# First two pairs of a 32-pair pipeline: W1 loaded first, adapters taken pair by pair, x2 ahead of the Q/K/V remainders

## The chip, the cores and the metric

One core of a Trainium2 chip. The metric is the device time of one execution in microseconds. The kernel before has a median of 950.8 over three runs (950.08 to 954.0).

## The reference

Four residual layers on x, 64 sequences of 64 tokens with 512 features, all in 32-bit floats. Only the first three matter here:

```python
x = x + einsum('bsi,bio->bso', x, W0[id]) + b0[id]           # one expert of 16 for each sequence
x = x + einsum('btd,od->bto', x, W1)                          # W1 and a low-rank adapter,
      + einsum('btr,bor->bto', einsum('btd,brd->btr', x, A[ad]), B[ad]) * s[ad]
x = x + attention(x)      # Q, K, V projections, RMS norm, rotation, a window of 256 old keys from a paged cache, Wo
x = x + einsum('bct,bcd->bdt', x, W3[subject]) + b3
```

## The kernel before

Two sequences make a pair of 128 rows, and 32 pairs go through two phases. Phase one computes the first two layers and Q, K and V, and stores x2, q and the new key and value rows; phase two does the attention and the last layer. Each engine has its own program, written out by hand, and runs it strictly in that order; semaphores tie them together. The first four pairs of phase one are written out without a loop.

In phase one, step k of an engine's program works on pair k and on the later parts of pair k-1 and k-2. For a pair:

- SP loads the two expert matrices, x, the bias and the rotation rows (`load_in`, for pair 0 `load_first`). All are issued on SP's one queue, in the order of the code. The loads of pair k wait for the expert products and the x1 of pair k-2.
- PE multiplies with the experts (`experts`, L602) into a bank. GpSimd (POOL) has summed x and bias (`sum_x_bias`, L461), and VectorE (DVE) adds both to x1 (`add_x1`, L1200).
- PE transposes x1 (L706). ScalarE (ACT) rounds it to x1t_hi (L926) and copies it to x1t (L927); DVE forms the remainder x1t_lo (L1234). A product with full precision is made of three: hi with hi, hi with lo, lo with hi.
- PE multiplies x1t with the two adapters' A (`adapt_down`, L623); ACT rounds that to xa_hi (L937) and DVE forms xa_parts (L1245). Then come the three W1 products (L728), four matmuls each, and one product with the adapters' B (L732), for which ACT has rounded pair_b to pair_b_hi (`round_adapters`, L893) and DVE has split it (`split_adapters`, L1212).
- DVE adds the sum to x1, which gives x2 (L1276). In the next step PE transposes x2 (L612), ACT rounds it (L919), DVE forms x2t_lo (L1205), and PE multiplies with the rounded Q, K and V weights and their remainders (L654 to L666).
- ACT squares q and k (L963, L964) and copies v; DVE sums, POOL takes the power (rms, L471), DVE and POOL rotate, PE transposes q.

ACT also loads pair_b and builds pair_a for a pair (`take_adapters`, L879 and L882): in the loop for pair k+2 at the end of step k. For pairs 0 and 1 it issues all four loads of pair_b ahead of step 0, behind the rounding of W1. Weights come into `stage` and are split once: ACT rounds W1 (L872) and Q, K, V (L942, L945), DVE forms the remainders w1_lo (L1229) and wqkv_lo (`split_inputs`, L1217). Before step 0 DVE also computes indices, the key bounds (L1074 to L1079) and the gains for the rotation tables (L1080 to L1084).

POOL's sum for the third pair (step 2) stands in step 2 behind the power and the rotation of the second; for later pairs it stands one step ahead.

`warm_up` (L584) are dummy matmuls of PE ahead of the first work and between its first pieces.

Of the kernel before, what the change touches and what calls it, by code (L numbers as in the profile page):

```python
# [4 lines left out]
F32 = mybir.dt.float32  # L5
# [43 lines left out]
WARM, WARM_X, WARM_T, WARM_Q, WARM_KEYS = 9, 6, 6, 24, 26  # L49
# [10 lines left out]
def build(nc, a):  # L60

    ctx = ExitStack()
    with ctx:
# [213 lines left out]
        def _(sp):  # L277

            sp.dma_start(ids_sb[:, :, :], a["ids"]).then_inc(ld_ids, 16)
            sp.dma_start(xt[:, 0, :, :], a["xt"][0]).then_inc(ld_xt[0], 16)  # L280
            sp.wait_ge(ld_ids, 16)
# [19 lines left out]
            def load_first():  # L301
# [15 lines left out]
                sp.dma_start(w1_stage, a["w1"]).then_inc(ld_w1, 16)  # L317
                sp.dma_start(lora_a[:, :, :], a["la"]).then_inc(ld_la, 16)
                sp.dma_start(wqkv_stage[:, :, 0:D], a["wq"]).then_inc(ld_wq, 16)
                sp.dma_start(wqkv_stage[:, :, D:D + 256], a["wk"]).then_inc(ld_wkv, 16)  # L320
                sp.dma_start(wqkv_stage[:, :, D + 256:], a["wv"]).then_inc(ld_wkv, 16)
                for h in range(2):
                    p0 = sp.value_load(ids_sb[0:1, 2, h:h + 1], min_val=0, max_val=NSLOT * BLK - T)
                    sp.dma_start(cs[T * h:T * h + T, 0, :], a["rope"][bass.ds(p0, T), :]).then_inc(ld_rope, 16)

# [249 lines left out]
        def _(pe):  # L575
# [51 lines left out]
            def project_inputs(k, s):  # L627

                if isinstance(k, int) and k == NP:
# [4 lines left out]
                    for ps_out, n0, done in ((ps_kv, D, kv_done), (ps_q, 0, qkv_done)):  # L634
# [7 lines left out]
                        last.then_inc(done, 1)  # L642
                elif on(k, 1, NP):
# [4 lines left out]
                    if isinstance(k, int) and k == 1:  # L648
                        pe.wait_ge(w_hi_ready, 2)
                    for ps_out, n0 in ((ps_q, 0), (ps_kv, D)):  # L650
                        if isinstance(k, int) and k == 1 and n0 == D:
                            pe.wait_ge(w_hi_ready, 3)
# [3 lines left out]
                    if isinstance(k, int) and k == 1:  # L656
                        pe.wait_ge(wqkv_lo_ready, 1)
                    for ps_out, n0 in ((ps_q, 0), (ps_kv, D)):
                        if n0 == D and on(k, 0, NP) and not (isinstance(k, int) and k == 1):
                            adapt_down(k, s)  # L660
                        if isinstance(k, int) and k == 1 and n0 == D:
                            pe.wait_ge(wqkv_lo_ready, 2)
# [17 lines left out]
            def phase_one(k, j, s):  # L680
# [35 lines left out]
                if on(k, 0, NP):  # L716

                    if isinstance(k, int) and k < 2:
                        adapt_down(k, s)
# [5 lines left out]
                    pe.wait_ge(x1lo_ready, k + 1)  # L725
                    for x_part, w_part in ((x1t_hi, w1_hi), (x1t_hi, w1_lo), (x1t_lo, w1_hi)):
                        for c in range(DC):
# [140 lines left out]
        def _(act):  # L868
            act.dma_start(numbers[:, :], a["numbers"]).then_inc(ld_small, 16)
            act.dma_start(reals[:, :], a["reals"]).then_inc(ld_small, 16)  # L870
            act.wait_ge(ld_w1, 16)
            nc.scalar.activation(w1_hi[:, :, :], w1_stage, ACT.Copy).then_inc(w_hi_ready, 1)  # L872

# [39 lines left out]
            def phase_one(k, j, s):  # L913
                r = 1 - s
                if on(k, 1, NP):
# [3 lines left out]
                    nc.scalar.activation(x2t_hi[:, :, :].rearrange("p c t -> p (c t)"), ps_t2[:, :], ACT.Copy).then_inc(x2hi_ready, 1)  # L919
                if on(k, 2, NP) and not (isinstance(k, int) and k == NP):  # L920
# [7 lines left out]
                if isinstance(k, int) and k == 0:  # L928
                    act.wait_ge(ld_la, 16)
                    for n in range(2):  # L930
                        take_adapters(n, n, load=False)
                    round_adapters(0, 0, 0)
# [5 lines left out]
                if on(k, -1, NP):  # L938
                    round_adapters(k + 1, j + s, 1 - s)
                if isinstance(k, int) and k == 0:  # L940
                    act.wait_ge(ld_wq, 16)
                    nc.scalar.activation(wqkv_hi[:, :, 0:D], wqkv_stage[:, :, 0:D], ACT.Copy).then_inc(w_hi_ready, 1)  # L942
                if isinstance(k, int) and k == 0:
                    act.wait_ge(ld_wkv, 2 * 16)
                    nc.scalar.activation(wqkv_hi[:, :, D:], wqkv_stage[:, :, D:], ACT.Copy).then_inc(w_hi_ready, 1)  # L945
# [22 lines left out]
                if on(k, -2, NP):  # L968
# [67 lines left out]
        def _(dve):  # L1036
# [37 lines left out]
            link(V.tensor_scalar(first_key[:, :], kvl_row[:, :], -1.0, float(WIN), ALU.mult, ALU.add))  # L1074
            link(V.tensor_scalar(first_key[:, :], first_key[:, :], fcols[:, TCOL:TCOL + 1], None, ALU.max))
            link(V.tensor_scalar(odd_i[:, :], kvl_row[:, :], 1, None, ALU.bitwise_and))
            link(V.tensor_scalar(odd[:, :], odd_i[:, :], 1.0, None, ALU.mult))
            link(V.tensor_tensor(first_key[:, :], first_key[:, :], odd[:, :], ALU.subtract))
            link(V.tensor_scalar(beyond[:, :], odd[:, :], BIG, None, ALU.mult))  # L1079
            link(V.tensor_scalar(gain_in[:, :, :], gain_in[:, :, :], 1.0, None, ALU.add))  # L1080
            for w, g in ((0, -1.0 / 16.0), (1, 1.0)):
                for f, half, sign in ((0, 0, 1.0), (1, 1, 1.0), (2, 1, -1.0), (3, 0, 1.0)):
                    link(V.tensor_scalar(gains[:, w, f, :], gain_in[:, w, 32 * half:32 * half + 32], g * sign, None, ALU.mult))
            V.tensor_copy(scol[:, 4:5], scol[:, 3:4]).then_inc(gains_ready, 1)  # L1084
# [351 lines left out]
```

## Time and profile before

| | us |
|---|---|
| median of three runs | 950.8 (950.08 to 954.0) |
| span of the profiled execution | 948.6 |
| PE busy | 907.5 (96%) |
| DVE busy | 651.1 (69%) |
| POOL busy | 522.3 (55%) |
| ACT busy | 444.3 (47%) |

Phase one ends at about 510 us of the profiled execution. Times in the rows are counted from the start of its span. Lines are those of the kernel before; behind a tile's name stands what it is made from. ACTq and SPq are instructions of the engine's own queue, mostly issues of loads. A bracket at the end of a row of the timeline tells how long the engine was idle ahead of it and what released it.

### The profile page before, as it was taken

To read this page: it belongs to the slowest core of one execution; us is meant where nothing else is said; L and a number is where in the kernel's file an instruction comes from. 1 tells how busy PE (TensorE), PEld (TensorE's weight loads), DVE (VectorE), ACT (ScalarE), POOL (GpSimd) and SP (SyncE) were. 2 spreads that over 40 slices of the span, in tenths; PEclk is the share of its full clock that TensorE was granted. 3 is DMA by queue.
4 is the path that set the end of the run, shared out by engine and by line. 5 is a ranking of instruction groups with operands and counts; after the bars stand their busy time and mean duration, and the time that the engine had idled before them with its cause. 6 is when DMAs were issued, how large, how long until landed. Compare 5 with 4: busy or idle time off the path is not lost.

```text
span 948.6 us, 23332 instructions
## 1 busy us (share of the span) xinstructions
PE 907.5 (96%) x6477; PEld 660.8 (70%) x6477; DVE 651.1 (69%) x1853; ACT 444.3 (47%) x1190; POOL 522.3 (55%) x502
## 2 busy tenths in 40 slices
PE   5789999999999999999997899999999999999997
PEld 3456666766666667666676777877777887787785
DVE  5345545667768774556754678777878877888875
ACT  2333333333333333333322566666666666666663
POOL 2136455464564657855556666566565665656530
PEclk9799999999999999999998799999999999999999
DMA  9978988778788787887844566666666676567741
GB/s 295 265 230 282 330 308 290 252 261 289 247 282 276 244 291 255 271 295 247 284 159 152 183 188 203 199 210 186 198 197 212 200 225 203 181 209 212 221 135 46
DMA packets 100413, 218.51 MB, mean 230 GB/s; under 512 B 30187, under 2 KB 36168, under 8 KB 92178
## 3 DMA queue, kind: packets, MB, share of 16 engines
q1 hardware_dynamic: 66290, 145.27, 47.0%
q0 software_dynamic: 25088, 57.74, 20.5%
q10 hardware_dynamic: 8992, 15.00, 4.9%
q8 instruction: 18, 0.29, 0.1%
q14 instruction: 25, 0.20, 0.1%
HBM read 210.39 MB, written 33.86 MB: 257 GB/s over the span
## 4 chain that ended last, share of the span: by engine, by line
PE 51%; POOL 18%; issue 15%; DMA 7%; SPq 4%; DVE 2%; ACT 1%; ACTq 1%; POOLq 0%; DVEq 0%
PE banks L823 9%; PE banks L775 9%; PE banks L811 7%; PE banks L798 6%; POOL rms L471 5%; DMA ring<-in_rope 5%; PE banks L752 4%; PE banks L859 3%; POOL ring L475 3%; POOL x_in L461 3%; PE banks L816 3%; POOL q_rot L480 2%; PE banks L753 1%; PE banks L791 1%; POOL ring L482 1%
## 5 line engine op out<-in xcount | busy, mean ns | idle before, releaser
L561 POOL DMA_INDIRECT ring<-new_rows,idx x128 | 129.4, 1011 | 82.5 <-PE banks L775 40.3
L471 POOL TENSOR_TENSOR rms<-ss,neg_half 128x12 f32<-128x12 f32 x31 | 70.8, 2284 | 185.4 <-DVE ss L1259 185.4
L992 ACT ACTIVATE big<-big,neg_max 128x320 f32<-128x320 f32 x256 | 141.4, 554 | 3.1 <-DVE neg_max L1317 2.7
L1317 DVE CUSTOM_DVE_ANT_0 big<-banks,mask 128x320 f32<-128x320 f32 x256 | 114.6, 486 | 27.4 <-PE banks L775 26.0
L602 PE MATMUL banks<-ring 128*64 128x512 f32 x512 | 117.8, 601 | 0.9 <-DMA ring<-in_w 0.9
L982 ACT ACTIVATE kt<-banks 128x384 f32<-128x384 f32 x128 | 61.8, 483 | 97.5 <-PE banks L753 97.5
L775 PE MATMUL banks<-kt,q_in 64*128 64x128 f32 (+2 forms) x768 | 88.6, 364 | 1.3 <-ACT kt L982 1.3
L550 POOL DMA_INDIRECT ring<-new_rows,idx x64 | 61.7, 965 | 47.0 <-PE banks L798 42.7
L1354 DVE TENSOR_SCALAR big<-big,recip 128x320 f32<-128x320 f32 x256 | 85.5, 396 | 2.3
L775 PEld LDWEIGHTS banks<-kt,q_in 64*128 64x128 f32 x768 | 74.4, 189 | 14.4 <-issue 8.4
L811 PEld LDWEIGHTS banks<-pt,ring 128*64 128x64 f32 x1024 | 55.4, 136 | 38.1 <-DVE pt L1299 25.4
L602 PEld LDWEIGHTS banks<-ring 128*64 128x64 f32 x512 | 34.1, 137 | 67.6 <-issue 66.8
L919 ACT ACTIVATE x2t_hi<-banks 128x512 fp32r<-128x512 f32 x32 | 19.1, 598 | 128.0 <-PE banks L612 128.0
L514 POOL DMA_INDIRECT ring<-in_kvrows,idx x64 | 61.2, 956 | 28.8 <-issue 13.5
L811 PE MATMUL banks<-pt,ring 128*64 128x128 f32 x1024 | 70.0, 278 | 2.7 <-DVE pt L1299 2.3
L664 PE MATMUL banks<-wqkv_hi,x2t_lo 128*128 128x512 f32 x248 | 70.4, 405 | 0.0
L798 PE MATMUL banks<-ident,big 128*128 128x128 f32 x512 | 67.4, 275 | 0.4 <-DVE ot_lo L1306 0.4
L654 PE MATMUL banks<-wqkv_hi,x2t_hi 128*128 128x512 f32 x248 | 66.6, 412 | 0.7 <-ACT x2t_hi L919 0.7
L666 PE MATMUL banks<-wqkv_lo,x2t_hi 128*128 128x512 f32 x248 | 66.6, 390 | 0.0
L1234 DVE TENSOR_TENSOR x1t_lo<-x1t,x1t_hi 128x512 fp32r<-128x512 f32 x32 | 40.3, 1258 | 35.9 <-ACT x1t L927 35.9
L1200 DVE TENSOR_TENSOR x<-banks,x_in 128x512 f32<-128x512 f32 x32 | 22.1, 691 | 55.6 <-PE banks L602 50.9
L798 PEld LDWEIGHTS banks<-ident,big 128*128 128x128 f32 x512 | 58.5, 142 | 1.0 <-DVE ot_lo L1306 0.9
(177 smaller groups left out, 1989.0 us busy)
## 6 DMA issues: line engine op xcount, KB each, us to landing
ring<-in_w SPq DMA_DIRECT2D x62, 1024.0 KB, 7.5
ring<-in_xt SPq DMA_DIRECT2D x32, 256.0 KB, 2.7
x_in<-in_x SPq DMA_DIRECT2D x32, 256.0 KB, 5.8
bias_in<-in_b SPq DMA_DIRECT2D x64, 128.0 KB, 6.4
x_dram<-x SPq DMA_DIRECT2D x32, 256.0 KB, 6.9
q_dram<-q_t ACTq DMA_DIRECT2D x32, 256.0 KB, 5.7
new_rows<-kv_out SPq DMA_DIRECT2D x32, 256.0 KB, 6.7
q_in<-q_dram SPq DMA_DIRECT2D x32, 256.0 KB, 2.7
```

The costliest lines, as they stand in the source:

```text
L471: nc.gpsimd.tensor_tensor(rms[:, s, :], ss[:, s, :], neg_half[:, :], ALU.pow).then_inc(rms_ready, 1)
L561: pool.indirect_dma_start(out=kv[:, s, c, :], out_offset=None, in_=new_rows, in_offset=bass.IndirectOffsetOnAxis(ap=idx[:, b, 1 + c:2 + c] ...
L602: last = nc.tensor.matmul(ps_l0[T * h:T * h + T, :], xt[:, s, c, T * h:T * h + T], w0[:, 2 * s + h, c * D:(c + 1) * D], start=(c == 0), st ...
L654: nc.tensor.matmul(ps_out[:, :], x2t_hi[:, c, :], wqkv_hi[:, c, n0:n0 + D], start=(c == 0), stop=False)
L664: nc.tensor.matmul(ps_out[:, :], x2t_lo[:, c, :], wqkv_hi[:, c, n0:n0 + D], start=False, stop=False)
L775: return nc.tensor.matmul(banks[:, S0[g] + n0:S0[g] + n1], q_in[r0:r0 + HD, s % 4, g // 2, :], kt[r0:r0 + HD, s % 2, g // 2, k0 + n0:k0 + ...
L798: last = nc.tensor.transpose(ps_pt[p][:, (q * 2 + c) * P:(q * 2 + c + 1) * P], prob[:, r % 2, (5 * p + 3 * q + c) * P:(5 * p + 3 * q + c + ...
L811: nc.tensor.matmul(ps_o[p][HD * q:HD * q + HD, :], kv[:, r, c, v0:v0 + HD], pt[:, p, PLACE[2 * p + q] % 2, c, :], start=(c == 0), stop=Fal ...
L823: last = nc.tensor.matmul(out[:, n0:n1], o_part[:, pair_s, c, :], w_part[:, c, n0:n1], start=(c == 0 and n == 0), stop=(c == DC - 1 and n ...
L992: nc.scalar.activation(prob[:, s % 2, PLACE[g] * NK:(PLACE[g] + 1) * NK], sm[:, s % 2, g, :], ACT.Exp, bias=neg_max[:, s % 2, g:g + 1], sc ...
L1317: V.tensor_tensor_reduce(sm[:, s % 2, g, :], ps_s[g], mask[:, s % 2, k0:k0 + NK], 1.0, 3.0e38, ALU.add, ALU.min, accum_out=neg_max[:, s % ...
L1354: V.tensor_scalar(own_row, own_row, recip[:, s % 2, g:g + 1], None, ALU.mult).then_inc(prob_ready, 1)
```

## The change

It touches the first pairs alone; the loop and phase two stay as they are.

- SP: W1's load is issued right behind the first x^T, ahead of the wait for the ids and of the expert weights. The rotation rows of pair 0 go ahead of K and V.
- ACT: the pair_b loads of pair 0 alone are issued at the start, then W1 is rounded, then pair 0's pair_b. In step 0 pair_a is built for pair 0 alone, and the Q weights are rounded ahead of xa_hi. In step 1, behind x2t_hi, ACT rounds K and V, loads and builds the adapters of pair 1 and rounds them, and loads and builds those of pair 2, all ahead of pair 1's x1t_hi.
- DVE: w1_lo goes ahead of the first x1; the key bounds move to step 3; the gains move into step 0 behind x1t_lo. Both weight splits and pair 1's adapter split move from step 0 behind x2t_lo in step 1, so x2 of pair 0 no longer stands behind them.
- PE: for pairs 0 and 1 the W1 products of x1t_hi come ahead of `adapt_down`, which comes ahead of those of x1t_lo. For pair 0's Q, K and V the products with the rounded weights come first and those with the remainders last. There are fourteen warm-up matmuls at the start instead of nine, and three instead of six behind the first x1 transposes.

DVE, from pair 0's x1 to its x2 and the remainder behind it (x is first x1, later x2), before:

```order
L1200 TENSOR_TENSOR x<-banks,x_in 128x512
L1229 TENSOR_TENSOR w_lo<-stage,w_hi 128x2048
L1234 TENSOR_TENSOR x1t_lo<-x1t,x1t_hi 128x512
L1212 TENSOR_TENSOR pair_b_parts<-pair_b,pair_b_hi 128x512
L1245 TENSOR_TENSOR xa_parts<-banks,xa_hi 64x64 x2
L1212 TENSOR_TENSOR pair_b_parts<-pair_b,pair_b_hi 128x512
L1217 TENSOR_TENSOR wqkv_lo<-stage,wqkv_hi 128x4x512
L1276 TENSOR_TENSOR x<-banks,x 128x512
L1205 TENSOR_TENSOR x2t_lo<-banks,x2t_hi 128x512
```

DVE in the same place, after, up to pair 1's x1 (the last row):

```order
L1216 TENSOR_TENSOR x<-banks,x_in 128x512
L1228 TENSOR_TENSOR pair_b_parts<-pair_b,pair_b_hi 128x512
L1251 TENSOR_TENSOR x1t_lo<-x1t,x1t_hi 128x512
L1096 TENSOR_SCALAR reals<-reals 128x128
L1099 TENSOR_SCALAR gains<-reals 128x32 x8
L1100 COPY scol<-scol 128x1
L1262 TENSOR_TENSOR xa_parts<-banks,xa_hi 64x64 x2
L1291 TENSOR_TENSOR x<-banks,x 128x512
L1221 TENSOR_TENSOR x2t_lo<-banks,x2t_hi 128x512
L1233 TENSOR_TENSOR wqkv_lo<-stage,wqkv_hi 128x4x512 x2
L1228 TENSOR_TENSOR pair_b_parts<-pair_b,pair_b_hi 128x512
L1216 TENSOR_TENSOR x<-banks,x_in 128x512
```

The second pair_b_parts (pair 1's) and the weight remainders moved from ahead of pair 0's x2 to behind it and ahead of pair 1's x1; the gains stand between x1t_lo and xa_parts.

ACT, step 1, from pair 0's x2t_hi to the squares of its q, before:

```order
L919 ACTIVATE x2t_hi<-banks 128x512
L926 ACTIVATE x1t_hi<-banks 128x512
L927 ACTIVATE x1t<-banks 128x512
L937 ACTIVATE xa_hi<-banks,reals 128x64
L893 ACTIVATE pair_b_hi<-pair_b,reals 128x512
L963 ACTIVATE sq<-banks 128x512
```

ACT from the same x2t_hi, after, through the first of four loads and builds of adapters, two for pair 1 and, behind pair 1's pair_b_hi, two for pair 2:

```order
L927 ACTIVATE x2t_hi<-banks 128x512
L930 ACTIVATE wqkv_hi<-stage 128x4x512
L883 TENSOR_LOAD ids_sb
L883 ISA x2
L885 ISA
L885 DMA pair_b<-in_lb 48x512
L888 ISA
L888 ACTIVATE pair_a<-lora_a,reals 128x4x48
```

ACT, after, from the last of these four to the squares:

```order
L885 DMA pair_b<-in_lb 48x512
L888 ISA
L888 ACTIVATE pair_a<-lora_a,reals 128x4x48
L940 ACTIVATE x1t_hi<-banks 128x512
L941 ACTIVATE x1t<-banks 128x512
L951 ACTIVATE xa_hi<-banks,reals 128x64
L899 ACTIVATE pair_b_hi<-pair_b,reals 128x512
L971 ACTIVATE sq<-banks 128x512
```

Between x2t_hi and x1t_hi there now stand the K/V rounding, four adapter loads with their builds, and a wait for the first two of them; pair 2's pair_b_hi, which stood ahead of the squares and still does, now takes loads that are issued in this same step.

The core of the diff:

```diff
-WARM, WARM_X, WARM_T, WARM_Q, WARM_KEYS = 9, 6, 6, 24, 26
+WARM, WARM_X, WARM_T, WARM_Q, WARM_KEYS = 14, 6, 3, 24, 26
...
             sp.dma_start(xt[:, 0, :, :], a["xt"][0]).then_inc(ld_xt[0], 16)
+            sp.dma_start(w1_stage, a["w1"]).then_inc(ld_w1, 16)
             sp.wait_ge(ld_ids, 16)
...
-                    if isinstance(k, int) and k < 2:
-                        adapt_down(k, s)
                     wait(pe, x2_ready, k)
...
                     for x_part, w_part in ((x1t_hi, w1_hi), (x1t_hi, w1_lo), (x1t_lo, w1_hi)):
+                        if isinstance(k, int) and k < 2 and x_part is x1t_lo:
+                            adapt_down(k, s)
+                            pe.wait_ge(x1lo_ready, k + 1)
...
             act.wait_ge(ld_ids, 16)
+            act.wait_ge(pb_set, 2)
+            take_adapters(0, 0, copy=False)
+            act.wait_ge(ld_w1, 16)
+            nc.scalar.activation(w1_hi[:, :, :], w1_stage, ACT.Copy).then_inc(w_hi_ready, 1)
             act.wait_ge(ld_small, 2 * 16)
-            act.wait_ge(pb_set, 2)
-            for k in range(2):
-                take_adapters(k, k, copy=False)
+            round_adapters(0, 0, 0)
...
+                if isinstance(k, int) and k == 1:
+                    act.wait_ge(ld_wkv, 2 * 16)
+                    nc.scalar.activation(wqkv_hi[:, :, D:], wqkv_stage[:, :, D:], ACT.Copy).then_inc(w_hi_ready, 1)
+                    take_adapters(1, 1)
+                    round_adapters(1, 0, 1)
+                    take_adapters(2, 0)
...
                 if isinstance(k, int) and k == 1:
                     split_x2(k)
+                    split_inputs(0)
                     split_inputs(1)
+                    split_adapters(1, 1)
...
                     if isinstance(k, int) and k == 0:
-                        split_adapters(0, 0)
+                        make_gains()
```

## Rows read from the trace of the kernel before

**Rows 1.** PE's waits, 60 to 505 us: total us, times, longest

```profile
PE banks L612 <- DVE x L1276: 2.2, 1, 2.2
PE banks L677 <- POOL q_rot L480: 2.1, 9, 0.6
```

**Rows 2.** Stretches: length, PE busy (instructions), granted clock, DMA share, GB/s

```profile
4.00:6.00 2.00, 1.59 (x7) 1.00 0.81 210
6.00:12.00 6.00, 5.19 (x21) 1.00 1.02 363
24.10:27.40 3.30, 3.30 (x12) 0.50 1.04 303
36.80:41.10 4.30, 4.30 (x10) 0.50 1.05 306
48.20:51.30 3.10, 1.14 (x20) 1.00 0.34 85
55.00:72.70 17.70, 15.74 (x87) 1.00 0.84 258
200.00:300.00 100.00, 99.14 (x544) 1.00 0.85 271
```

**Rows 3.** Timeline of PE, start and length in us, instruction, [idle before <-releaser]

```profile
17.21 0.66 PE L706 MATMUL banks<-ident,x 128*128 128x128 f32 x4 [1.70 <-DVE x L1200]
...
28.52 0.39 PE L732 MATMUL banks<-pair_b_parts,xa_parts 128*128 128x512 f32 x1
34.99 1.11 PE L612 MATMUL banks<-ident,x 128*128 128x128 f32 x4 [6.08 <-DVE x L1276]
...
50.82 0.69 PE L623 MATMUL banks<-x1t,pair_a 128*64 128x64 f32 x16 [1.22 <-issue]
...
56.24 3.65 PE L602 MATMUL banks<-ring 128*64 128x512 f32 x16
...
62.88 0.66 PE L706 MATMUL banks<-ident,x 128*128 128x128 f32 x4 [1.96 <-DVE x L1200]
```

**Rows 4.** Timeline of DVE

```profile
13.58 2.76 DVE L1083 TENSOR_SCALAR gains<-reals 128x32 f32<-128x32 f32 x8
...
30.12 0.69 DVE L1212 TENSOR_TENSOR pair_b_parts<-pair_b,pair_b_hi 128x512 fp32r<-128x512 f32 x1 [2.45 <-ACT pair_b_hi L893]
31.92 2.29 DVE L1217 TENSOR_TENSOR wqkv_lo<-stage,wqkv_hi 128x2048 fp32r<-128x2048 f32 x1 [1.11 <-ACT wqkv_hi L942]
34.24 0.69 DVE L1276 TENSOR_TENSOR x<-banks,x 128x512 f32<-128x512 f32 x1
```

**Rows 5.** Timeline of ACT and its queue (ACTq)

```profile
18.05 3.45 ACTq L879 DMA_DIRECT2D pair_b<-in_lb  x4
21.54 0.60 ACT L926 ACTIVATE x1t_hi<-banks 128x512 fp32r<-128x512 f32 x1 [2.56 <-issue]
...
29.36 0.72 ACT L893 ACTIVATE pair_b_hi<-pair_b,reals 128x512 fp32r<-128x512 f32 x1 [2.59 <-DMA pair_b<-in_lb]
29.99 1.89 ACT L942 ACTIVATE wqkv_hi<-stage 128x2048 fp32r<-128x2048 f32 x1
30.05 1.50 ACTq L879 DMA_DIRECT2D pair_b<-in_lb  x2
...
51.75 0.71 ACT L893 ACTIVATE pair_b_hi<-pair_b,reals 128x512 fp32r<-128x512 f32 x1
```

**Rows 6.** Timeline of POOL

```profile
14.61 1.26 POOL L461 TENSOR_TENSOR x_in<-x_in,bias_in 128x512 f32<-128x512 f32 x1 [5.97 <-DMA bias_in<-in_b]
...
60.78 1.26 POOL L461 TENSOR_TENSOR x_in<-x_in,bias_in 128x512 f32<-128x512 f32 x1
```

**Rows 7.** Landing of pair_b loads (L879): that issued at 31.2; all 17 to 130

```profile
DMA to landing us min/median/max: 8.2/8.2/8.2
...
DMA to landing us min/median/max: 5.0/6.2/8.2
```

**Rows 8.** Landing of the expert matrix (L292) issued at 22.8

```profile
DMA to landing us min/median/max: 14.1/14.1/14.1
```

More of the change, by code:

```diff
@@ L642, in project_inputs @@
                         last.then_inc(done, 1)
+                elif isinstance(k, int) and k == 1:
+                    pe.wait_ge(x2hi_ready, 1)
+                    for i, (ps_out, n0) in enumerate(((ps_q, 0), (ps_kv, D))):
+                        pe.wait_ge(w_hi_ready, 2 + i)
+                        for c in range(DC):
+                            nc.tensor.matmul(ps_out[:, :], x2t_hi[:, c, :], wqkv_hi[:, c, n0:n0 + D], start=(c == 0), stop=False)
+                        pe.wait_ge(x2lo_ready, 1)
+                        for c in range(DC):
+                            nc.tensor.matmul(ps_out[:, :], x2t_lo[:, c, :], wqkv_hi[:, c, n0:n0 + D], start=False, stop=False)
+                    for i, (ps_out, n0) in enumerate(((ps_q, 0), (ps_kv, D))):
+                        pe.wait_ge(wqkv_lo_ready, 1 + i)
+                        for c in range(DC):
+                            last = nc.tensor.matmul(ps_out[:, :], x2t_hi[:, c, :], wqkv_lo[:, c, n0:n0 + D], start=False, stop=(c == DC - 1))
+                    last.then_inc(qkv_done, 1)
                 elif on(k, 1, NP):
@@ L929, in phase_one @@
                     act.wait_ge(ld_la, 16)
-                    for n in range(2):
-                        take_adapters(n, n, load=False)
-                    round_adapters(0, 0, 0)
+                    take_adapters(0, 0, load=False)
+                    act.wait_ge(ld_wq, 16)
+                    nc.scalar.activation(wqkv_hi[:, :, 0:D], wqkv_stage[:, :, 0:D], ACT.Copy).then_inc(w_hi_ready, 1)
                 if on(k, 0, NP):
@@ L937, in phase_one @@
                     nc.scalar.activation(xa_hi[:, :], ps_la[:, 0:T], ACT.Copy, scale=fcols[:, XPART:XPART + 1]).then_inc(xa_hi_ready, 1)
-                if on(k, -1, NP):
+                if on(k, -1, NP) and not (isinstance(k, int) and k == 0):
                     round_adapters(k + 1, j + s, 1 - s)
[L940 to L945, printed above, removed]
                 if on(k, 2, NP) and not (isinstance(k, int) and k == NP):
@@ L967, in phase_one @@
                     nc.scalar.activation(kv_out[:, r, 256:512], ps_kv[:, 256:512], ACT.Copy).then_inc(sqv_ready, 1)
-                if on(k, -2, NP):
+                if on(k, -2, NP) and not (isinstance(k, int) and k == 0):
                     take_adapters(k + 2, s)
@@ L1073, in _ @@
                 link(V.tensor_scalar(xa_parts[T * h:T * h + T, T - T * h:P - T * h], mrow[T * h:T * h + T, 0:T], 0.0, None, ALU.mult))
[L1074 to L1083, printed above, removed]
@@ L1086, in take_tables, with make_gains @@
+            def make_gains():
+                link(V.tensor_scalar(gain_in[:, :, :], gain_in[:, :, :], 1.0, None, ALU.add))
+                for w, g in ((0, -1.0 / 16.0), (1, 1.0)):
+                    for f, half, sign in ((0, 0, 1.0), (1, 1, 1.0), (2, 1, -1.0), (3, 0, 1.0)):
+                        link(V.tensor_scalar(gains[:, w, f, :], gain_in[:, w, 32 * half:32 * half + 32], g * sign, None, ALU.mult))
+                V.tensor_copy(scol[:, 4:5], scol[:, 3:4]).then_inc(gains_ready, 1)
             def take_tables():
@@ L1246, in phase_one @@
                     last.then_inc(xa_ready, 1)
-                if on(k, -1, NP):
+                if on(k, -1, NP) and not (isinstance(k, int) and k == 0):
                     split_adapters(k + 1, r)
-                if isinstance(k, int) and k == 0:
-                    split_inputs(0)
                 if isinstance(k, int) and k == NP:
```

35 lines of the change are left out of this document (16 added, 19 removed).

## The prediction

> **What bounds the kernel now.** I read the waits of the tensor engine (PE) first, then its busy time and granted clock by stretch, then the timelines of the first 63 us on each engine, then the landing times of single loads. From 60 to 505 us PE waits 2.2 us on one x2 add and 2.1 us in nine small waits on q_rot [rows 1], and from 200 to 300 us it is busy 99.14 of 100 us at full clock [rows 2]. So phase one is bound by PE once it runs, and a microsecond won or lost before that reaches the end of phase one as it is. The loads, the attention phase and the stores behind it hang on PE's progress, and nothing there has a date of its own. The question is only when the steady run begins. Its first instruction is the transpose of the third pair's x1 at 62.88, before which PE stood 1.96 us for the DVE add [rows 3]; from there it does not stop. I follow what sets that date.
>
> Two stretches come before it. **The first pair's x2** is added at 34.24, though its last product L732 started at 28.52 and took 0.39 [rows 3, 4]. In between DVE stood in program order behind pair 1's split (30.12, after 2.45 us of waiting for ACT's rounding, which itself waited for a load until 29.36) and behind a 2.29 us weight split [rows 4, 5]. **The third pair's start** is late for another reason: from the ACT rounding of pair 2's adapter at 51.75 a chain of ACT squares, DVE sums, the POOL power and rotation, and POOL's x + bias at 60.78 leads to 62.88 without a gap that the change touches [rows 5, 6]. That chain is 62.88 - 51.75 = 11.1 us long, and it stays.
>
> **The change, part by part.** W1's load goes ahead of the expert weights. It is 128 x 2048 words, 1.05 MB; at the 363 GB/s of 6 to 12 us that would hold the rest back by 2.9 us, but from 4 to 6 us only 210 GB/s moved [rows 2], so 0.3 MB (0.85 us) fits into room that is empty now, and it is issued before the wait for the ids. Ends: 0 and 2.9 us; I take 1.7. The bias then lands at 16.3 instead of 14.6, and POOL's sum of 1.26 [rows 6] ends at 17.55. Against it DVE no longer has the gains in front of x1: the row from 13.58 is 2.76 us long [rows 4] and ended about half a microsecond after POOL's sum did. Pair 0's x1 is added at 17.6, and its transposes start at 18.35 instead of 17.21 [rows 3]: a loss of 1.1 us.
>
> Then the gain begins. ACT issued four adapter loads, 3.45 us from 18.05, and was late with x1t_hi because of that: it rounded at 21.54 after transposes that ended at 17.9 [rows 3, 5]. After the change two loads were issued long before; x1t_hi runs from 19.05 to 19.65. PE takes the eight rounded W1 products at once; twelve such products took some 3.3 us at half clock [rows 2], so at full clock they are no bound. DVE has x1t_lo until about 20.9 and then the moved gains, 2.76 plus about 0.4 for the instruction on each side, to 24.1. ACT rounds the Q weights in 1.89 us [rows 5], is done by about 23.3, and has xa_hi at 23.6. So xa_parts waits for the gains: the cover that hid them is gone and they cost about half a microsecond here. xa_parts at 24.1 to 24.6, L732 0.39 [rows 3], x2 added from 25.05 to 25.75: **9.2 us earlier than 34.24** [rows 4]. The transposes end at 26.5.
>
> This is not what reaches the end. Pair 1's adapter loads, issued before 21.5 now, move behind x2t_hi and the K/V rounding on ACT, so they start from that 26.5. When ACT was released at 29.36, the two loads behind it took 1.50 us from 30.05 [rows 5], so the second was issued at 31.2, 1.85 us after the release. Here: 28.35. That load landed after 8.2 us [rows 7], with the same queue of expert weights ahead of it as it will have here, so pair 1's pb_hi can start at 36.55. Behind this wait stand, on ACT, the loads for pair 2, x1t_hi of pair 1 and all that follows; on DVE, pair 1's split and its x1 add. Pair 2's second load then goes out 1.85 us after 36.55, at 38.4. Of seventeen such loads the shortest took 5.0, the median 6.2 and the longest 8.2 [rows 7]; the queue is still loaded then, so I take 7.0, between median and longest. Pair 2's rounding starts at 45.4 instead of 51.75: **6.3 us earlier**. The chain of 11.1 us brings the steady start to 56.5.
>
> By the Trainium skill (DMA: Bandwidth & Descriptors, "Queues, rings and completion order"), each DMA engine takes turns between the queue rows that have work, a packet from each, so a small load on ACT's row should not stand behind what SP has queued; the same page's "Anatomy of one DMA — SWDGE (gpsimd) path" puts the fixed cost at about 2 us. By that the two landings would be an estimated 2 to 3 us each and this chain no bound at all. The trace disagrees with 5.0 as the shortest of 17 and 8.2 beside a full SP queue.
>
> The other path to pair 2's rounding is PE's. Pair 1's second expert matrix was issued at 22.8 and landed 14.1 us later, at 36.9 [rows 8]; the earlier start of the queue brings that to about 35.4. Q/K/V of pair 0 are ready before that: rounding K/V from 26.6 takes two times 1.89 at most, the two splits on DVE 2.29 each [rows 4, 5], which gives about 33. Expert products 3.65 [rows 3], x1, transposes, x1t_hi, eight W1 products and the adapter product: xa_hi at 44.0. That is 1.4 us before the landing, so it is not the later one, but it is the floor: faster loads gain at most 51.75 - 44.0 = 7.75 us.
>
> What is late next is PE's clock. Pair 2's expert products, from 56.24 now, will be done by about 49.5, and until 56.5 PE has eight transposes. The clock was full from 55 to 72.7. From 48.2 to 51.3 PE was busy 1.14 us, and behind that the clock stood at its lower level (1.2 instead of 2.4 GHz); the unbroken work from 24.1 to 27.4 and from 36.8 to 41.1 also ran at 0.50 before the clock rose [rows 2]. Half of such a stretch is lost, 1.65 to 2.15 us; I take 1.8. Bounds 0 (it does not fall) and 2.15.
>
> The rest costs nothing: the key bounds move to step 3, where DVE waits for ACT's xa_hi anyway; W1's remainder split fits behind the index arithmetic, before x1; fourteen warm-ups instead of nine lie inside the later landing of the expert weights; three fewer behind the transposes free PE for x1t_hi; rope ahead of K/V moves 0.07 MB. Sum: -6.3 + 1.8 = **-4.5 us**. The profiled execution goes from a span of 948.6 to 944.1, and since the median of the three runs is 950.8, 2.2 above that span, I predict 946.3. A half per cent is 4.75 us, about what a measurement of this kernel can tell from no change.
>
> **The rivals.** Short landings: the adapter loads take the trace's shortest times, sum near 11 instead of 15.2. PE's path then binds (from a sum of 13.8 down), -7.75 + 1.8 = -5.95, 944.9. The turn-taking in the Trainium skill's page on DMA would end here too. For this rival speaks that ACT's queue is its own; against it the 8.2 [rows 7]. No fall of the clock: -6.3, 944.5; against it the fall after 48.2. A later x2: the W1 load holds the first pair back by its full 2.9 us (1.2 more) and both landings are at 8.2 (1.2 more), -2.1, 948.7. Slower: the two adapter landings are in series where they were issued ahead of need, and each delays ACT and through it everything. The gain is gone when their sum is 15.2 + 4.5 = 19.7 us and half a per cent is lost at 24.4, 12 us each (955.5). The longest seen is 8.2 for one, but large SP loads took 14.1 in the same stretch [rows 8]. That the change does not reach the end at all (phase one bound elsewhere) has PE's 99.14 of 100 us against it and is part of the slow case.
>
> **How the numbers follow.** Forecast 0.45, short landings 0.18, clock stays 0.07, later x2 0.22, slower 0.08. The forecast lies 0.25 us inside the half per cent, so a little under half of it counts as faster: 0.20 + 0.18 + 0.07 = 0.45 faster; 0.25 + 0.22 + 0.02 = 0.49 same; 0.06 slower. The range runs from PE's floor with the clock kept (-7.75: 943.0) to a gain of 0.8 (950.0), which leaves out most of the slower case and the tail of the later x2.
>
> **What would show it.** Right: x1t_hi of pair 0 near 19 and its x2 near 25; ACT idle until about 36.5 before pair 1's pb_hi, and again until about 45.4 before pair 2's, both released by the pair_b load; POOL's power following by some 3 us; PE with a hole of several us before the third pair's x1 transposes and half clock behind it; then no wait of PE over 1 us in phase one. Wrong: pb_hi released by PE or by nothing, no hole ahead of the third pair, or PE waiting again later in phase one.

## The result and the profile after

The kernel after the change takes 943.9 us (median of four times, 941.1 to 944.8). The four times of the kernel before on record beside it have a median of 950.8, 7.0 us more; the ratio on record is 0.9908 [0.9881, 0.9935], which is 8.7 us, 6.2 to 11.3. A second comparison (a2_after) gives 942.2 against 953.0, 0.9887 [0.9863, 0.9912], 10.8 us. The forecast was 946.3, a gain of 4.5. The time lies in the range, at its lower end; the gain is 1.6 to 2.4 times the forecast, and "no change that can be measured" had the larger share of the chances. The profiled span went from 948.6 to 941.5, by 7.1.

The start of the kernel after, first POOL's first sum (start and length in us, instruction, [idle before <-releaser]), which answers to the first of [rows 6]:

```profile
16.28 1.27 POOL L461 TENSOR_TENSOR x_in<-x_in,bias_in 128x512 f32<-128x512 f32 x1 [7.88 <-DMA bias_in<-in_b]
```

DVE, where the gains now stand (beside [rows 4]):

```profile
17.65 0.69 DVE L1216 TENSOR_TENSOR x<-banks,x_in 128x512 f32<-128x512 f32 x1 [3.73 <-POOL x_in L461]
...
21.07 1.69 DVE L1099 TENSOR_SCALAR gains<-reals 128x32 f32<-128x32 f32 x8
...
24.02 0.69 DVE L1291 TENSOR_TENSOR x<-banks,x 128x512 f32<-128x512 f32 x1 [0.60 <-PE banks L741]
```

ACT and its queue, from the first pair's x2t_hi to the third pair's adapter (beside [rows 5]):

```profile
25.45 0.60 ACT L927 ACTIVATE x2t_hi<-banks 128x512 fp32r<-128x512 f32 x1 [2.52 <-PE banks L612]
...
26.13 1.51 ACTq L885 DMA_DIRECT2D pair_b<-in_lb  x2
...
34.73 0.72 ACT L899 ACTIVATE pair_b_hi<-pair_b,reals 128x512 fp32r<-128x512 f32 x1 [6.19 <-DMA pair_b<-in_lb]
35.75 0.33 ACTq L885 DMA_DIRECT2D pair_b<-in_lb  x1
...
36.93 0.33 ACTq L885 DMA_DIRECT2D pair_b<-in_lb  x1
...
41.59 0.31 ACT L951 ACTIVATE xa_hi<-banks,reals 128x64 fp32r<-128x64 f32 x1 [2.40 <-PE banks L623]
44.11 0.72 ACT L899 ACTIVATE pair_b_hi<-pair_b,reals 128x512 fp32r<-128x512 f32 x1 [2.20 <-DMA pair_b<-in_lb]
```

The two new waits are there, 6.19 and 2.20 us, both released by the pair_b load, and the second one sets the date: the xa_hi of the same engine is through by 41.9. The four loads, and a fifth issued at 44.79, landed in 6.7 to 7.4 us:

```profile
DMA to landing us min/median/max: 6.7/7.2/7.4
```

PE, first the second pair's expert products, then the third pair (beside the end of [rows 3]):

```profile
32.98 3.65 PE L602 MATMUL banks<-ring 128*64 128x512 f32 x16 [0.56 <-DMA ring<-in_w]
...
49.82 0.66 PE L612 MATMUL banks<-ident,x 128*128 128x128 f32 x4 [2.54 <-DVE x L1291]
51.86 1.11 PE L684 MATMUL banks<-ident,q_rot 128*128 128x128 f32 x4 [1.38 <-POOL q_rot L480]
55.23 1.12 PE L713 MATMUL banks<-ident,x 128*128 128x128 f32 x4 [2.26 <-DVE x L1216]
...
66.59 3.65 PE L602 MATMUL banks<-ring 128*64 128x512 f32 x16
```

and its stretches there (length, PE busy with instructions, granted clock, DMA share, GB/s), beside [rows 2]:

```profile
4.00:6.00 2.00, 1.76 (x8) 1.00 0.94 375
6.00:12.00 6.00, 3.86 (x26) 1.00 1.00 355
48.00:52.00 4.00, 0.80 (x5) 0.95 1.00 297
52.00:56.00 4.00, 1.74 (x8) 0.50 0.22 68
56.00:60.00 4.00, 4.00 (x15) 0.69 0.88 274
60.00:64.00 4.00, 4.00 (x31) 1.00 1.03 352
```

The third pair's x1 transposes moved from 62.88 to 55.23, by 7.65 us. In front of them PE is busy 0.80 of 4 us and then 1.74 of 4, and the clock goes to its lower level (1.2 instead of 2.4 GHz) for about 7 us (0.50 in every microsecond from 52 to 58, and parts of the two beside them). The expert products of the fourth pair, the first work behind that stretch, moved from 72.74 to 66.59, by 6.15; so the clock took 1.50 back. Behind it PE waits as little as before [rows 1]: from 60 to 505 us

```profile
PE banks L612 <- DVE x L1291: 2.2, 1, 2.2
PE banks L684 <- POOL q_rot L480: 2.2, 10, 0.4
PE banks L639 <- ACT x2t_hi L927: 0.7, 1, 0.7
```

### The profile page after: what moved, and what is told of

It is laid out like the page before. It is cut to its first block, busy times and chain, and to the rows that moved or that the text cites. A ratio compares the mean times of both kernels' runs of the same rounds, so it can differ in the third digit from the quotient of the medians.

```text
span 941.5 us, 23334 instructions
## 1 busy us (share of the span) xinstructions
PE 901.8 (96%) x6481; PEld 655.9 (70%) x6481; DVE 649.5 (69%) x1853; ACT 445.2 (47%) x1190; POOL 520.1 (55%) x502
## 4 chain that ended last, share of the span: by engine, by line
PE 52%; POOL 20%; issue 15%; DMA 5%; SPq 2%; DVE 2%; ACT 1%; ACTq 0%; POOLq 0%; DVEq 0%
PE banks L832 9%; PE banks L784 9%; PE banks L820 7%; PE banks L807 6%; POOL rms L471 6%; PE banks L761 4%; POOL ring L475 3%; PE banks L868 3%; POOL x_in L461 3%; POOL q_rot L480 3%; PE banks L825 3%; DMA ring<-in_rope 2%; DMA pair_b<-in_lb 2%; PE banks L671 2%; POOL ring L494 1%
## 5 line engine op out<-in xcount | busy, mean ns | idle before, releaser
L561 POOL DMA_INDIRECT ring<-new_rows,idx x128 | 129.4, 1011 | 81.6 <-PE banks L784 45.4
L820 PEld LDWEIGHTS banks<-pt,ring 128*64 128x64 f32 x1024 | 55.3, 136 | 38.3 <-DVE pt L1314 26.1
L514 POOL DMA_INDIRECT ring<-in_kvrows,idx x64 | 61.2, 956 | 28.7 <-issue 13.5
L671 PE MATMUL banks<-wqkv_hi,x2t_lo 128*128 128x512 f32 x240 | 67.9, 404 | 0.0
L673 PE MATMUL banks<-wqkv_lo,x2t_hi 128*128 128x512 f32 x240 | 64.4, 390 | 0.0
L665 PE MATMUL banks<-wqkv_hi,x2t_hi 128*128 128x512 f32 x240 | 64.0, 409 | 0.0
```

What stands on the lines that cost most here:

```text
L561: pool.indirect_dma_start(out=kv[:, s, c, :], out_offset=None, in_=new_rows, in_offset=bass.IndirectOffsetOnAxis(ap=idx[:, b, 1 + c:2 + c] ...
L671: nc.tensor.matmul(ps_out[:, :], x2t_lo[:, c, :], wqkv_hi[:, c, n0:n0 + D], start=False, stop=False)
L673: last = nc.tensor.matmul(ps_out[:, :], x2t_hi[:, c, :], wqkv_lo[:, c, n0:n0 + D], start=False, stop=(c == DC - 1))
L820: nc.tensor.matmul(ps_o[p][HD * q:HD * q + HD, :], kv[:, r, c, v0:v0 + HD], pt[:, p, PLACE[2 * p + q] % 2, c, :], start=(c == 0), stop=Fal ...
```

## The experiments

All dates come from one profile of each kernel. A span falls into four pieces in every one of these traces: the start, up to the fourth pair's expert products; the steady run, up to the transposes of the last x2; the turn into phase two, up to the eighth transposes of keys (L752 before, L761 after); and the rest. Over all fourteen traces the steady run takes 427.3 to 428.2 us and the rest 410.0 to 410.5. The turn takes 34.9 to 40.3, and two traces of one kernel differ there by up to 2.5. So a change in the first pairs is read at the first two columns, and the span carries the turn's scatter besides.

| kernel | third pair's x1 transposes | fourth pair's experts | turn | span |
|---|---|---|---|---|
| before, as shown | 62.88 | 72.74 | 38.0 | 948.6 |
| before, b2_before | 66.52 | 76.37 | 35.9 | 950.5 |
| before, b3_before | 65.93 | 77.41 | 38.4 | 954.0 |
| after, as shown | 55.23 | 66.59 | 37.6 | 941.5 |
| after, a2_after | 54.89 | 66.76 | 38.3 | 942.6 |
| e1_loads_early | 55.33 | 68.00 | 34.9 | 940.8 |
| e2_sum_ahead | 53.17 | 64.04 | 37.1 | 939.2 |
| e3_fill | 55.20 | 65.04 | 35.7 | 938.4 |
| e4_x2_late | 57.31 | 69.59 | 38.4 | 945.6 |
| e5_before_dve | 65.09 | 76.38 | 40.3 | 955.2 |
| e6_w1_back | 60.86 | 73.24 | 36.2 | 947.4 |
| e8_loads_step0 | 53.92 | 65.96 | 38.3 | 941.7 |
| e9_step0_sum | 51.41 | 61.20 | 39.7 | 939.1 |
| e9b_step0_sum | 50.78 | 60.57 | 40.1 | 938.6 |

My theory: the landings of the adapter loads, one after the other on ACT, set the third pair's date; a fixed chain of about 11 us and the clock follow. The rivals: PE's own path or the x2 of the first pair sets it, or the order on DVE alone does.

**The loads issued early.** All four loads for the first two pairs go out at the start again, the rest of the change stays:

```diff
-            take_adapters(0, 0, copy=False)
+            for k in range(2):
+                take_adapters(k, k, copy=False)
...
-                    take_adapters(1, 1)
+                    take_adapters(1, 1, load=False)
...
-                    take_adapters(2, 0)
...
```

The loads for pair 2 go back to the end of step 0, behind a wait for the first split.

> The changed kernel with one part undone: ACT issues the pair_b loads of pairs 0 and 1 together at the start, and those of pair 2 at the end of step 0, as before the change; the rest of the change stays. Theory (two adapter landings in series set the third pair's start): ACT no longer waits for a load in step 1; pair 2's pb_hi follows xa_hi of pair 1 at about 41.8 instead of 44.1, PE's x1 transposes of the third pair start near 53 instead of 55.2, and the span falls by about 2 us. Rival (the loads were not the bound, taking them pair by pair is what won time because ACT's queue is short): the x1 transposes at 55.2 or later, span the same or longer.

Both adapter waits went, and the date did not move (55.33). ACT in this kernel:

```profile
30.10 0.71 ACT L899 ACTIVATE pair_b_hi<-pair_b,reals 128x512 fp32r<-128x512 f32 x1
43.99 0.31 ACT L951 ACTIVATE xa_hi<-banks,reals 128x64 fp32r<-128x64 f32 x1 [2.40 <-PE banks L623]
44.20 0.71 ACT L899 ACTIVATE pair_b_hi<-pair_b,reals 128x512 fp32r<-128x512 f32 x1
```

and PE's second expert products, which started at 32.98 in the kernel after:

```profile
35.37 3.65 PE L602 MATMUL banks<-ring 128*64 128x512 f32 x16 [1.29 <-DMA ring<-in_w]
```

The last rounding now comes right behind xa_hi, at 44.20 instead of 44.11. The 0.2 MB of adapters ahead of the bias and the expert weights moved POOL's first sum from 16.28 to 17.79 and the second experts by 2.4 us. The expectation counted only the wait that goes, and not what the loads hold up: PE's path came in at the same date. This run alone doesn't tell the theory from its first rival; the next ones do.

**The loads issued in step 0.** Here the loads for pair 1 stand at the end of step 0, behind the first pair's loads but ahead of its x2:

```diff
-                if on(k, -2, NP) and not (isinstance(k, int) and k == 0):
+                if isinstance(k, int) and k == 0:
+                    take_adapters(1, 1)
+                elif on(k, -2, NP):
                     take_adapters(k + 2, s)
...
```

In step 1 those for pair 2 follow a wait for the first split and stand ahead of pair 1's rounding.

> The changed kernel with the adapter loads moved one place ahead on ACT without touching the start: pair 1's are issued at the end of step 0, behind xa_hi, where ACT stands idle from 22.9 to 25.4, and pair 2's behind the K/V rounding, ahead of the wait for pair 1's. The first loads stay as changed. Theory (the second landing is the bound of the third pair's start, and what kept the run with the loads at the very start from winning was 0.2 MB more ahead of the first bias): x1 of pair 0 stays at 17.65, pb_hi of pair 2 starts right behind xa_hi of pair 1 at 41.8 instead of 44.1, PE's x1 transposes of the third pair near 52.9 instead of 55.2, the span about 2 us shorter. Rival (ACT's own order or the issue of loads eats it): 55 or later.

The date came 1.3 us earlier (53.92). ACT:

```profile
24.55 0.33 ACTq L885 DMA_DIRECT2D pair_b<-in_lb  x1
...
33.99 0.72 ACT L899 ACTIVATE pair_b_hi<-pair_b,reals 128x512 fp32r<-128x512 f32 x1 [5.26 <-DMA pair_b<-in_lb]
42.59 0.31 ACT L951 ACTIVATE xa_hi<-banks,reals 128x64 fp32r<-128x64 f32 x1 [2.40 <-PE banks L623]
42.80 0.71 ACT L899 ACTIVATE pair_b_hi<-pair_b,reals 128x512 fp32r<-128x512 f32 x1
```

The second landing is off the path (42.80 right behind xa_hi), as the theory has it, and PE's path is the next bound, 1.3 us below. Here too that path came later than in the kernel after, with the second experts at 33.97 instead of 32.98, and of the 1.3 us 0.6 are left at the fourth pair's experts (65.96 against 66.59). Of pair 1's two loads the second went out 2.75 us earlier than in the kernel after (24.55 against 27.3) and was there only 0.74 earlier: 9.4 us instead of 7.4. The first, also 2.75 us earlier (23.38 against 26.13), kept most of its lead: 7.2 instead of 6.9.

**x2 late again.** The Q/K/V remainder goes back ahead of the first pair's x2:

```diff
                     split_x2(k)
-                    split_inputs(0)
                     split_inputs(1)
...
+                if isinstance(k, int) and k == 0:
+                    split_inputs(0)
```

> The changed kernel with one part undone on DVE: the split of the Q weights goes back ahead of pair 0's x2. That delays x2 by about 1.7 us (the split takes 2.3, and its weights are rounded at 22.7). Theory (x2, the issue of the adapter loads behind it, two landings and the POOL chain are one series): the third pair's x1 transposes start 1.7 us later, near 56.9, and the span is 1.7 us longer than the changed kernel's. Rival (there is slack behind x2): they start within 0.5 us of 55.2.

ACT, x2t_hi of the first pair and pair 1's rounding:

```profile
27.29 0.60 ACT L927 ACTIVATE x2t_hi<-banks 128x512 fp32r<-128x512 f32 x1 [4.44 <-PE banks L612]
...
37.94 0.72 ACT L899 ACTIVATE pair_b_hi<-pair_b,reals 128x512 fp32r<-128x512 f32 x1 [7.57 <-DMA pair_b<-in_lb]
```

x2t_hi came 1.84 us later (27.29), pair 1's rounding waited 7.57 us for its load until 37.94, and the third pair's date is 57.31, 2.08 later. So x2 counts by way of what ACT issues behind it.

**The order on DVE alone**, in the kernel before: both splits moved behind x2t_lo, nothing else.

```diff
                     split_x2(k)
+                    split_inputs(0)
                     split_inputs(1)
+                    split_adapters(1, 1)
...
-                if on(k, -1, NP):
+                if on(k, -1, NP) and not (isinstance(k, int) and k == 0):
                     split_adapters(k + 1, r)
-                if isinstance(k, int) and k == 0:
-                    split_inputs(0)
```

> The kernel before with one part of the change alone: on DVE the Q weight split and pair 1's adapter split go behind x2t_lo, so that pair 0's x2 no longer stands behind them. Theory (x2 early is of use only with ACT's order changed as well): x2 is added near 29.0 instead of 34.2, but x2t_hi stands on ACT behind the Q and K/V rounding and the builds for pair 2 until about 34.5 (36.1 before), so the third pair's x1 transposes start near 61.2 instead of 62.9 and the span falls by 1.6 us. Rival (the DVE order alone carries the gain): they start near 57 or earlier.

DVE, x2 and the remainder behind it:

```profile
31.80 0.69 DVE L1276 TENSOR_TENSOR x<-banks,x 128x512 f32<-128x512 f32 x1 [2.33 <-PE banks L732]
38.13 0.69 DVE L1205 TENSOR_TENSOR x2t_lo<-banks,x2t_hi 128x512 fp32r<-128x512 f32 x1 [5.64 <-ACT x2t_hi L919]
```

x2 was added at 31.80, and then DVE stood 5.64 us for ACT's x2t_hi. In the profile shown of before it was at 34.24, but this run's first sum began at 16.74 instead of 14.61; two more traces of before begin like it, with x2 at 37.31 and 37.45 (below). Against those x2 is 5.6 us earlier and the third pair's date 65.09, 0.8 to 1.4 earlier; the 61.2 that was expected had been reckoned from the early start. x2 by itself is worth little as long as ACT's roundings stand where they stood.

**W1 loaded where it was**, the rest of the change kept:

```diff
-            sp.dma_start(w1_stage, a["w1"]).then_inc(ld_w1, 16)
             sp.wait_ge(ld_ids, 16)
...
+                sp.dma_start(w1_stage, a["w1"]).then_inc(ld_w1, 16)
                 sp.dma_start(lora_a[:, :, :], a["la"])
```

> The changed kernel with one part undone: W1's load goes back behind the first expert weights, bias and identity. Theory: W1 lands near 17, ACT rounds it until 19, DVE, which now has W1's remainder ahead of x1 in its order, adds x1 of pair 0 near 21.3 instead of 17.65, and all that follows is about 3.7 us later: the third pair's x1 transposes near 59, the span 3.5 to 4 us longer than the changed kernel's. Rival (W1 first is a loss of 1.1 us that the rest could do without): x1 near 16.5 and a span no longer than the changed kernel's.

POOL's first sum and, on DVE, the W1 remainder with the x1 behind it:

```profile
16.55 1.26 POOL L461 TENSOR_TENSOR x_in<-x_in,bias_in 128x512 f32<-128x512 f32 x1 [8.10 <-DMA bias_in<-in_b]
```

```profile
21.05 2.29 DVE L1083 TENSOR_TENSOR w_lo<-stage,w_hi 128x2048 fp32r<-128x2048 f32 x1 [9.43 <-ACT w_hi L905]
23.26 0.68 DVE L1216 TENSOR_TENSOR x<-banks,x_in 128x512 f32<-128x512 f32 x1
```

The date went to 60.86, 5.6 us later and not 3.7, since W1 itself came later than reckoned: ACT's rounding of it began at 19.04, where 17 was expected. Of the parts undone here this one costs the most, because the new order on DVE has the W1 remainder ahead of x1; what W1 first would give with the old order is not tested. And the bias did not land earlier with W1 out of its way: 16.55 against 16.28. That was not what I had reckoned, and it asked for more traces of both kernels.

**Both kernels again**, unchanged:

> The kernel before, unchanged, to see how far its first 70 us differ from run to run: pair 0's bias landed at 14.6 in the first trace, but at 16.6 to 16.7 in two later kernels whose loads had W1 in the old place. Theory (the first trace had an early start; W1 first costs little): bias near 16.6, the third pair's x1 transposes near 64.5 to 65, the span 950 or more. Rival (14.6 is what the old order gives, W1 first costs 1.7 us): bias at 14.6 within 0.3 us and the transposes at 62.9 within 0.5.

> The same kernel once more, for the same question: a second value of the bias landing and of the third pair's start. If the two differ by more than 1 us, the start is scattered by the memory system, and no single trace prices W1's place.

> The changed kernel, unchanged, with more rounds. Theory: the third pair's x1 transposes at 55.2 within 0.5, the span 939 to 943 depending on the clock at the start of phase two, the ratio to the kernel before between 0.990 and 0.9935 (6 to 9.5 us).

POOL's first sum in the two traces of before and the one of after, in this order:

```profile
16.53 1.26 POOL L461 TENSOR_TENSOR x_in<-x_in,bias_in 128x512 f32<-128x512 f32 x1 [8.07 <-DMA bias_in<-in_b]
```

```profile
16.65 1.26 POOL L461 TENSOR_TENSOR x_in<-x_in,bias_in 128x512 f32<-128x512 f32 x1 [8.06 <-DMA bias_in<-in_b]
```

```profile
16.22 1.27 POOL L461 TENSOR_TENSOR x_in<-x_in,bias_in 128x512 f32<-128x512 f32 x1 [7.31 <-DMA bias_in<-in_b]
```

The 14.61 of [rows 6] does not come back, and the third pair is later than the 64.5 to 65 expected of b2_before. With W1 behind the expert weights the sum starts at 14.61 once and at 16.53 to 16.74 in four traces (two of before, e5, e6); with W1 first, at 16.06 to 16.40 in eight traces (and at 17.79 in e1, behind the adapters). From the late start the kernel before runs late throughout: its third pair's transposes are at 66.52 and 65.93 instead of 62.88, and of its 11 times in that comparison the lowest is 948.5 and the median 953.0. Against these two traces the change brings about 11 us at the third pair (66.2 to 55.1, means of two) and about 10 us of span (952.3 to 942.1), and the ratio of a2_after (0.9887) lies below the 0.990 to 0.9935 that was expected. The four late traces were taken on two chips. On which chip the early one was taken is not on record, so it is open whether the start differs from execution to execution or from chip to chip.

**POOL's sum a step ahead**, in the kernel after: the third pair's x + bias in step 1, like the later ones.

```diff
-                if isinstance(k, int) and k == 2:
-                    sum_x_bias(2, 1, 0)
...
-                if on(k, -1, NP) and not (isinstance(k, int) and k == 1):
+                if on(k, -1, NP):
```

> The changed kernel with POOL's x + bias of the third pair moved from step 2 to step 1, where POOL is idle from 36.8 to 47.1 us. Theory (the third pair's x1 stands behind the POOL chain of power and rotation by program order alone): x1 of the third pair is added when its expert products are done, near 47.5, and PE's transposes of it follow those of q at about 52.5 instead of 55.2; about 2.5 us less. Rival (the loads of pair 2 land late, or PE's order keeps the date): POOL stands waiting for the bias, the power starts later than 47.1, and nothing is won.

POOL's sum of the third pair:

```profile
44.56 1.27 POOL L461 TENSOR_TENSOR x_in<-x_in,bias_in 128x512 f32<-128x512 f32 x1 [8.64 <-DMA ring<-in_rope]
```

The date is 53.17, 2.06 earlier: POOL, which stood idle for 8.64 us ahead of this sum, is done with it before the power at 47.53. So the tail of the 11 us chain is work in POOL's order, and not a fixed cost. PE's transposes of q (L682 here) and of x1 now stand back to back:

```profile
52.26 1.12 PE L682 MATMUL banks<-ident,q_rot 128*128 128x128 f32 x4 [1.39 <-POOL q_rot L480]
53.17 1.06 PE L711 MATMUL banks<-ident,x 128*128 128x128 f32 x4
```

**The hole filled.** Nineteen dummy matmuls in PE's step 2, in the waits ahead of the third pair's x1 (8 behind the experts, 4 behind the x2 transposes, 7 behind those of q):

```diff
+                    if isinstance(k, int) and k == 2:
+                        fill(8)
...
```

> The changed kernel with 19 more dummy matmuls of PE in its hole ahead of the third pair's x1 transposes (8, 4 and 7). Theory (the fall of the clock in that hole costs 1.5 us): the clock stays at its upper level from 48 to 64 us, x1 transposes still start near 55.2, and the third expert products after them start near 65.1 instead of 66.6. Rival (the clock's fall lies in time that was idle anyway, or the dummies hold PE up): the products at 66.6 or later.

```profile
48.00:52.00 4.00, 3.10 (x27) 1.00 1.00 309
52.00:56.00 4.00, 2.84 (x24) 1.00 0.17 54
56.00:60.00 4.00, 4.00 (x32) 1.00 0.86 270
```

The clock stays at its upper level, the date is the same (55.20), and the fourth pair's experts come 1.55 us earlier. That is the 1.50 read above as the clock's share, from the other side.

**Loads in step 0 and the sum ahead together**, run twice, the second time for its time:

> The kernel with the adapter loads one place ahead on ACT and, besides, POOL's x + bias of the third pair in step 1. Theory (the two waits are in series): x1 transposes of the third pair near 50.5, the third pair's successor's expert products near 61 instead of 66.6, the span 5 us shorter than the changed kernel's 941.5. Rival (the two removals share their gain): not below the 53.2 that the sum alone gave.

> The kernel with the adapter loads one place ahead on ACT and POOL's x + bias of the third pair in step 1, timed. Theory: the third expert products after the transposes stay at 61.2, 5.4 us ahead of the changed kernel's 66.6, and since phase one is bound by PE the time falls by about as much on average: ratio to the kernel before 0.985 to 0.9885. Rival (what is won before the steady run is given back at the start of phase two): the same ratio as the changed kernel's within 0.001.

The dates are 51.41 and 50.78, the clock stays up without dummies, and the fourth pair's experts are 5.4 to 6.2 us earlier than in the kernel after. The turn took about 2 us of that back in these two traces (39.7 and 40.1). The time is 940.1 (936.2 to 942.4), ratio to before 0.9864 [0.9834, 0.9894]: 2.0 us below the kernel after in the same comparison (942.2), with intervals that overlap. So the time did not fall by as much as the start, as had been expected; that the turn gives back a part of any earlier start is a rival that two traces with its scatter do not rule out. It is the lowest median seen here, and its lead over the kernel after is not beyond doubt.

## Why the prediction missed

**The path was right; two sizes in the sum were not.** Every step that was named came, in its order: the first pair's x2 ahead of the splits, two landings in series on ACT, POOL's chain, the hole in PE, the lower clock, and no new wait behind it. Not one rival took its place. But the sum came to 4.5 us, just inside the half per cent, and the gain is 7.0 to 10.8.

*The first step that failed* is the price of W1's load: "Ends: 0 and 2.9 us; I take 1.7. The bias then lands at 16.3 instead of 14.6". It landed at 16.28, so in the time itself, 943.9 where 946.3 was forecast, this term has no part. But the 14.6 is that of one trace out of five: in the four others with W1 in its old place the sum began at 16.53 to 16.74. Against those, W1 first costs the bias nothing and gives about 0.4 us (16.25, the mean of the eight, against 16.62, the mean of the four), which is outside the bounds. Loading W1 also brought 375 and 424 GB/s from 4 to 6 us (after, a2_after) where before and its two other traces moved 202 to 224.

The late start reaches the third pair by way of ACT and the loads. ACT's rounding of W1 in before and in b2_before:

```profile
17.07 1.91 ACT L872 ACTIVATE w_hi<-stage 128x2048 fp32r<-128x2048 f32 x1 [14.15 <-DMA stage<-in_w]
```

```profile
18.98 1.91 ACT L872 ACTIVATE w_hi<-stage 128x2048 fp32r<-128x2048 f32 x1 [16.06 <-DMA stage<-in_w]
```

It is 1.91 us later, pair 1's last adapter load behind it took 9.3 us instead of 8.2, and the first pair's x2 is 3.07 later; the third pair is 3.1 to 3.6 later in the two late traces. How often a timed run of before starts late is not known. About 1.8 us lie around the span in each run (943.3 for 941.5, 952.3 for 950.5), so the profiled execution took about 950.4, and three of the four times beside the result are like it (950.1 to 950.9). So this step is behind what goes beyond the 7.1 us between the two profiles: 1.6 us by the ratio of the first comparison, 3.7 in the second. That the late start makes this difference is argued from the traces; the timed runs do not show their start.

*The second step that failed* is the cost of the moved gains, the largest of the terms that were mis-sized.

All terms, against the profile shown, where 4.5 us were forecast and 7.1 came:

| term | forecast | measured |
|---|---|---|
| first x1 transposes | 18.35 | 18.40 |
| gains in front of xa_parts | 2.76 | 1.69 |
| x2 of the first pair | 25.05 | 24.02 |
| pair 1's second load issued, landing | 28.35, 8.2 | 27.3, 7.4 |
| pair 1's rounding | 36.55 | 34.73 |
| from there to pair 2's second load | 1.85 | 2.20 |
| its landing | 7.0 | 7.2 |
| pair 2's rounding | 45.4 | 44.11 |
| chain to the third pair's x1 transposes | 11.1 | 11.12 |
| these transposes | 56.5 | 55.23 |
| loss by the clock | 1.8 | 1.50 |

Of the gains, [rows 4] shows eight instructions in 2.76 us, and I carried that over as their cost. The median of the eight is 182 ns. One took 1244, beside POOL's first sum, and nothing of the kind stands beside them in their new place. Seen by instruction (duration ns min, median, max), before and after:

```profile
L1083 DVE TENSOR_SCALAR gains<-reals x8: 181/182/1244, 13.6 to 16.2; 128x32 f32<-128x32 f32 x8
```

```profile
L1099 DVE TENSOR_SCALAR gains<-reals x8: 180/181/182, 21.1 to 22.6; 128x32 f32<-128x32 f32 x8
```

That is 1.05 of the 1.27 us by which the third pair's date beat the forecast; the first landing gave 0.8 more, and the longer issue and the second landing took about half a microsecond of it back. The clock gave 0.3 more. Another 0.9 comes behind the start: 0.1 in the steady run, 0.5 in the turn and 0.4 in the rest. The first two are less than traces of one kernel differ by; the third is most of the 0.5 us by which that piece varies over the fourteen traces, and stays unexplained. One reading was wrong without effect: the twelve instructions from 24.1 to 27.4 were eight W1 products and the end of an adapter product.

**The floor of PE's path** was put at 44.0 and measured 41.6, since pair 1's experts began at 32.98 and ran through; the landing of the second expert matrix, counted on for 35.4, did not hold them. The conclusion that the landings come last stood by a wider margin (2.5 us) than reckoned. With the loads early (e1) or in step 0 (e8) that path is next, at 44.2 and 42.8.

**The rivals.** Short landings: no, 6.7 to 7.4 us in the kernel after. By the Trainium skill (DMA: Bandwidth & Descriptors, "Queues, rings and completion order") each DMA engine takes turns between the queue rows that have work. Whether that should have kept these loads clear of SP's the runs do not settle: in e8 one load of the pair lost most of its lead and the other kept it, and in e6, where SP had issued nothing since 37.22, pair 2's loads at 42.42 and 43.60 landed in 3.0 and 3.9 us. The clock stays: not in the kernel after, only with PE's waits filled (e3) or shortened (e9). Later x2: no, 24.02. Slower by serial landings: their sum was 14.6, where 19.7 would have been needed.

**The chances.** "Same" had 0.49, since the forecast lay just inside the half per cent, and the range reached to 943.0 on the strength of PE's floor. What the chances lacked is a case in which the one profile of the kernel before is not typical of its start; its median, 0.4 us above what the profiled execution took, gave no sign of that, and only more profiles did.

## What to carry to other kernels

Before a date of a profile that depends on loads goes into a sum, take a second profile of the same kernel: here the first sum began two microseconds earlier in one trace than in four others, and a price read from it alone has no error bar. A row that groups instructions hides a blocked one; the median of one instruction times their number is the cost to carry to a new place. When a wait is taken away, look what the load that is moved for it now stands ahead of (e1, where the second experts came 2.4 us later): put a late-needed load behind the bytes that the first product needs and ahead of the instruction that waits (e8).

## What the runs showed of the hardware

- One DVE instruction of 128x32 took 1244 ns instead of 181 beside a POOL sum of 1.26 us that began at 14.61; in b2_before, where the gains were over before that sum began at 16.53, all eight took 181 or 182 ns. The Trainium skill (SBUF — State Buffer, "Who interferes with whom") says that VectorE in certain modes and GpSimd share a port pair that one holds for the whole instruction while the other blocks. The 1244 ns fit that, since both ended at about 15.9; no run here shows in which mode the instruction ran.
- A 96 KB adapter load took 6.7 to 7.4 us beside SP's queue in the kernel after and up to 9.4 us in e8. In e6 two of them took 3.0 and 3.9 us, where the DMA engines were busy for 0.58 (42 to 44 us) and 0.30 (44 to 46) of the time; in the kernel after the share was 1.0 or more from 26 to 44 us.
- The turn between the phases took 34.9 to 40.3 us over these kernels, and the granted clock goes with it: taken over the turn itself it was 0.90 to 0.95 in the four traces below 36.3 us (0.95 in b2_before) and 0.74 to 0.79 in the three above 39.5 (0.74 in e9b_step0_sum). What makes the clock differ there is not shown.
- Why the first loads of the kernel before landed two microseconds earlier in one trace out of five with that order stays open. In that trace 363 GB/s moved from 6 to 12 us [rows 2] against 328 and 326 in the two others of the kernel; that is seen, and what held them back is not.
